# Two score steps in one: attention and feed-forward of 32 sequences on one core, with TensorE's order laid anew

## The reference

```
Q, K, V = x Wq' + bq, x Wk' + bk, x Wv' + bv          # 16 heads of 8 channels
scores  = Q K' / sqrt(8); above the diagonal -inf; plus -(i - j)
attn    = softmax(scores) V, then Wo and bo
x       = layernorm(x + attn)
h       = silu(w1 x * s1) * (w2 x * s2)               # 128 -> 512, ternary weights with a scale per row
h       = gelu(h1 h * s); h = gelu(h2 h * s)          # 512 -> 512, twice
x       = layernorm(x + w3 h * s)                     # 512 -> 128
```

## Time and profile before

| | |
|---|---|
| median of 3 executions | 780.16 us (778.53 to 780.32) |
| span of the profiled execution | 776.4 us |
| TensorE busy, share of the span | 729.4 us, 94% |
| VectorE | 598.0 us, 77% |
| ScalarE | 554.2 us, 71% |
| GpSimd | 509.5 us, 66% |
| mean granted TensorE clock | 0.959 |

### The profile page before, as it was taken

How to read it: one execution, slowest core, us unless ns; L and a number is a source line. 1 busy time by engine, 2 the same in 40 slices (tenths; PEclk the granted TensorE clock), 3 DMA queues, 4 the chain that set the end, 5 groups by cost and what they waited for, 6 DMA issues and landing times. The chain is left out here.

```text
span 776.4 us, 19033 instructions
## 1 busy us (share of the span) xinstructions
PE 729.4 (94%) x6025; PEld 497.7 (64%) x6025; DVE 598.0 (77%) x2759; ACT 554.2 (71%) x876; POOL 509.5 (66%) x616
## 2 busy tenths in 40 slices
PE   3798999999999999999999999999999999999895
PEld 1476466676766666676766667676766667676663
DVE  3978688797878889797888879797877979786242
ACT  5255558768595977869596877869596776959684
POOL 4145575858577585857677584857758585757764
PEclk8567899999999999999999999999999999999998
DMA  6511310303121120313122030312121030310100
GB/s 207 200 32 35 109 37 18 131 30 118 44 106 55 60 88 17 129 33 117 46 102 58 22 127 16 126 37 110 51 88 59 18 128 21 115 33 22 26 1 29
DMA packets 55213, 54.36 MB, mean 70 GB/s; under 512 B 27816, under 2 KB 35304, under 8 KB 55112
## 3 DMA queue, kind: packets, MB, share of 16 engines
q1 hardware_dynamic: 55112, 53.12, 21.0%
HBM read 12.20 MB, written 4.19 MB: 21 GB/s over the span
## 5 line engine op out<-in xcount | busy, mean ns | idle before, releaser
L969 DVE CUSTOM_DVE_ANT_0 ps<-ps,causal 128x256 f32<-128x256 f32 (+1 forms) x928 | 297.5, 393 | 26.1 <-PE ps L646 24.3
L1116 POOL TENSOR_SCALAR_AFFINE_SELECT pt<-pt 128x512 f32<-128x512 f32 x256 | 160.4, 636 | 105.0 <-ACT pt L819 100.0
L1163 POOL TENSOR_TENSOR hlo<-hf,hhi 128x512 fp32r<-128x512 f32 x128 | 164.0, 1287 | 95.7 <-ACT hhi L903 94.3
L819 ACT ACTIVATE pt<-ps 128x768 f32<-128x768 f32 x256 | 194.9, 808 | 31.1 <-PE ps L686 28.1
L893 ACT ACTIVATE hf<-ps,vec_sb 128x512 f32<-128x512 f32 x128 | 86.2, 684 | 99.6 <-PE ps L604 99.6
L598 PE MATMUL ps<-hhi,h_hi 128*128 128x512 f32 x496 | 146.3, 416 | 0.4 <-ACT hhi L903 0.3
L604 PE MATMUL ps<-hlo,h_hi 128*128 128x512 f32 x496 | 138.7, 398 | 1.7 <-POOL hlo L1169 0.7
L969 DVE DVE_READ_ACCUMULATOR2_ANT m<- 128x1 f32 x928 | 131.0, 141 | 0.0
L604 PEld LDWEIGHTS ps<-hlo,h_hi 128*128 128x128 f32 x496 | 93.4, 188 | 28.0 <-POOL hlo L1169 5.9
L703 PE MATMUL ps<-pt,vst 128*32 128x256 f32 (+1 forms) x2048 | 105.7, 335 | 0.1
L598 PEld LDWEIGHTS ps<-hhi,h_hi 128*128 128x128 f32 x496 | 85.3, 188 | 20.9 <-ACT hhi L903 0.7
(11 more groups left out here) (116 smaller groups left out, 1115.5 us busy)
## 6 DMA issues: line engine op xcount, KB each, us to landing
ks<-k_hi SPq DMA_DIRECT2D x30, 256.0 KB
qs<-q_hi SPq DMA_DIRECT2D x30, 256.0 KB
xT<-in_x SPq DMA_DIRECT2D x16, 256.0 KB, 2.8
x_tok<-in_xtok SPq DMA_DIRECT2D x16, 256.0 KB, 2.8
num<-raw SPq DMA_DIRECT2D x64, 64.0 KB, 2.0
den<-sums SPq DMA_DIRECT2D x128, 32.0 KB, 1.8
out<-o_tok SPq DMA_DIRECT2D x16, 256.0 KB, 2.2
ks<-k_lo SPq DMA_DIRECT2D x15, 256.0 KB
```

Of the source, the lines that this page charges most:

```text
L819: nc.scalar.activation(pt[u][:, c:c + 2, :], ps[:, first:last + 1, 0:3 * P], ACT.Exp).then_inc(t_free.sem, 1)
L969: part = nc.vector.tensor_tensor_reduce(ps[:, bank, cols], ps[:, bank, cols], mask, 1.0, LOWEST, ALU.add, ALU.max, m32[b][:, it, c + e, u: ...
L1116: nc.gpsimd.affine_select(out=diag, in_=diag, compare_op=ALU.is_ge, fill=0.0, base=0, pattern=[[0, 2], [0, 2], [1, P]], channel_multiplier ...
L1163: nc.gpsimd.tensor_tensor(h_lo[layer % 2][:, m, :], hf[:, n % 4, :], h_hi[layer % 2][:, m, :].bitcast(F32), ALU.subtract).then_inc(hlo_rea ...
```

## The change

Every even score step is joined with the next odd one. `s2` b, n stands for `s` n and n+1, `st2` b, n for `st` n and n+1. The four heads lie in four different groups of 32 partitions and four banks. All four wide products come first, then the four narrow ones; after the second narrow product the signal for step n is given, after the fourth that for n+1. Before the first product stands the wait that step n+1 had, so both pairs of banks must be free. In `st2` and also in the single `st` the wide product now comes before the narrow one. In the slot all 32 steps are joined to 16; in the fill some are. In `PE_ORDER` the other steps are placed anew around them: `h` 1,0 stands before `s2` 0,2, `mT` 0 behind `s2` 1,0, `x1t` directly behind `s2` 1,2, `qq` directly behind `s2` 1,4, and `pv` 0,2 and 0,3 side by side. Nothing is changed on the other engines.

```diff
 PE_ORDER = [
-    ("u", 3, -2), ("s", 0, 0, 0), ("s", 0, 1, 0), ("pv", 1, 2, -1), ("pv", 1, 3, -1), ("s", 0, 2, 0),
-    ("h", 1, 0, -2), ("s", 0, 3, 0), ("s", 0, 4, 0), ("h", 1, 1, -2), ("h", 1, 2, -2), ("s", 0, 5, 0),
-    ("s", 0, 6, 0), ("h", 1, 3, -2), ("s", 0, 7, 0), ("wo", -1), ("s", 1, 0, 0), ("h", 2, 0, -2), ("mT", 0, 0),
-    ("s", 1, 1, 0), ("s", 1, 2, 0), ("h", 2, 1, -2), ("s", 1, 3, 0), ("h", 2, 2, -2), ("s", 1, 4, 0),
-    ("s", 1, 5, 0), ("x1t", -1), ("h", 2, 3, -2), ("s", 1, 6, 0), ("s", 1, 7, 0), ("qq", 1), ("g", 0, -1),
-    ("u", 0, -1), ("w3h", -2), ("st", 0, 0, 0), ("st", 0, 1, 0), ("qk", 1), ("w3l", -2), ("st", 0, 2, 0),
-    ("st", 0, 3, 0), ("u", 1, -1), ("g", 1, -1), ("mT", 1, 0), ("st", 0, 4, 0), ("st", 0, 5, 0),
-    ("pv", 0, 0, 0), ("pv", 0, 1, 0), ("st", 0, 6, 0), ("st", 0, 7, 0), ("zt", 2, -2), ("g", 2, -1),
-    ("u", 2, -1), ("st", 1, 0, 0), ("st", 1, 1, 0), ("pv", 0, 2, 0), ("st", 1, 2, 0), ("g", 3, -1),
-    ("pv", 0, 3, 0), ("st", 1, 3, 0), ("st", 1, 4, 0), ("qv", 1), ("st", 1, 5, 0), ("pv", 1, 0, 0),
-    ("st", 1, 6, 0), ("st", 1, 7, 0), ("pv", 1, 1, 0),
+    ("u", 3, -2), ("s2", 0, 0, 0), ("pv", 1, 2, -1), ("pv", 1, 3, -1), ("h", 1, 0, -2), ("s2", 0, 2, 0),
+    ("h", 1, 1, -2), ("h", 1, 2, -2), ("s2", 0, 4, 0), ("h", 1, 3, -2), ("wo", -1), ("s2", 0, 6, 0),
+    ("h", 2, 0, -2), ("h", 2, 1, -2), ("s2", 1, 0, 0), ("mT", 0, 0), ("h", 2, 2, -2), ("s2", 1, 2, 0),
+    ("x1t", -1), ("h", 2, 3, -2), ("s2", 1, 4, 0), ("qq", 1), ("g", 0, -1), ("u", 0, -1), ("s2", 1, 6, 0),
+    ("w3h", -2), ("st2", 0, 0, 0), ("qk", 1), ("w3l", -2), ("st2", 0, 2, 0), ("u", 1, -1), ("g", 1, -1),
+    ("mT", 1, 0), ("st2", 0, 4, 0), ("pv", 0, 0, 0), ("pv", 0, 1, 0), ("st2", 0, 6, 0), ("zt", 2, -2),
+    ("g", 2, -1), ("u", 2, -1), ("st2", 1, 0, 0), ("pv", 0, 2, 0), ("pv", 0, 3, 0), ("st2", 1, 2, 0),
+    ("g", 3, -1), ("qv", 1), ("st2", 1, 4, 0), ("pv", 1, 0, 0), ("st2", 1, 6, 0), ("pv", 1, 1, 0),
 ]
...
-                        elif kind == "s":
+                        elif kind in ("s", "s2"):
                             _, b, n = s
-                            u, banks = n // 2, SCORE[n % 2]
+                            steps_of = (n,) if kind == "s" else (n, n + 1)
...
-                            wait_max_banks(pe, HP * b + n, q)
+                            wait_max_banks(pe, HP * b + steps_of[-1], q)
                             heads = []
-                            for e, bank in enumerate(banks):
-                                c = 2 * (n % 2) + e
...
+                            for i in steps_of:
+                                for e, bank in enumerate(SCORE[i % 2]):
+                                    c = 2 * (i % 2) + e
...
-                            for bank, qr, kr in heads:
-                                last = pe.matmul(ps[:, bank, T:T + P], qr[:, 0:P], kr[:, 0:P], start=False,
+                            for h, (bank, qr, kr) in enumerate(heads):
+                                part = pe.matmul(ps[:, bank, T:T + P], qr[:, 0:P], kr[:, 0:P], start=False,
                                                  stop=True, skip_group_check=True)
-                            last.then_inc(s_full.sem, 1)
+                                if h % 2:
+                                    part.then_inc(s_full.sem, 1)
...
-                        elif kind == "st":
+                        elif kind in ("st", "st2"):
...
-                            wait_exp_banks(pe, HP * b + n, q)
+                            wait_exp_banks(pe, HP * b + steps_of[-1], q)
...
-                                pe.matmul(ps[:, bank, 0:P], kr[:, P:T], qr[:, P:T], start=True, stop=False,
+                            for bank, qr, kr in heads:
+                                pe.matmul(ps[:, bank, P:P + T], kr[:, 0:P], qr, start=True, stop=False,
                                           skip_group_check=True)
-                                last = pe.matmul(ps[:, bank, P:P + T], kr[:, 0:P], qr, start=False,
+                            for h, (bank, qr, kr) in enumerate(heads):
+                                part = pe.matmul(ps[:, bank, 0:P], kr[:, P:T], qr[:, P:T], start=False,
                                                  stop=True, skip_group_check=True)
-                            last.then_inc(t_full.sem, 1)
+                                if h % 2:
+                                    part.then_inc(t_full.sem, 1)
```

More of the change, by code:

```diff
@@ L634, in run @@
                                 stacked.wait(pe, q - 1)
-                            wait_max_banks(pe, HP * b + n, q)
+                            wait_max_banks(pe, HP * b + steps_of[-1], q)
                             heads = []
-                            for e, bank in enumerate(banks):
-                                c = 2 * (n % 2) + e
-                                rows = slice(32 * c, 32 * c + 32)
-                                heads.append((bank, qs[p][rows, u, b * T:(b + 1) * T],
-                                              ks[p][rows, u, b * T:(b + 1) * T]))
+                            for i in steps_of:
+                                for e, bank in enumerate(SCORE[i % 2]):
+                                    c = 2 * (i % 2) + e
+                                    rows = slice(32 * c, 32 * c + 32)
+                                    heads.append((bank, qs[p][rows, i // 2, b * T:(b + 1) * T],
+                                                  ks[p][rows, i // 2, b * T:(b + 1) * T]))
                             for bank, qr, kr in heads:
@@ L672, in run @@
                             last.then_inc(mT_full.sem, 1)
-                        elif kind == "st":
+                        elif kind in ("st", "st2"):
                             _, b, n = s
-                            u, banks = n // 2, SCORE[n % 2]
+                            steps_of = (n,) if kind == "st" else (n, n + 1)
                             if n == 0:
                                 m_sent.wait(pe, q, 2 * b + 2)
-                            wait_exp_banks(pe, HP * b + n, q)
[L679 to L682, removed]
-                                pe.matmul(ps[:, bank, 0:P], kr[:, P:T], qr[:, P:T], start=True, stop=False,
+                            wait_exp_banks(pe, HP * b + steps_of[-1], q)
+                            heads = []
+                            for i in steps_of:
+                                for e, bank in enumerate(SCORE[i % 2]):
+                                    c = 2 * (i % 2) + e
+                                    rows = slice(32 * c, 32 * c + 32)
+                                    heads.append((bank, qs[p][rows, i // 2, b * T:(b + 1) * T],
+                                                  ks[p][rows, i // 2, b * T:(b + 1) * T]))
+                            for bank, qr, kr in heads:
+                                pe.matmul(ps[:, bank, P:P + T], kr[:, 0:P], qr, start=True, stop=False,
                                           skip_group_check=True)
-                                last = pe.matmul(ps[:, bank, P:P + T], kr[:, 0:P], qr, start=False,
+                            for h, (bank, qr, kr) in enumerate(heads):
+                                part = pe.matmul(ps[:, bank, 0:P], kr[:, P:T], qr[:, P:T], start=False,
                                                  stop=True, skip_group_check=True)
-                            last.then_inc(t_full.sem, 1)
+                                if h % 2:
+                                    part.then_inc(t_full.sem, 1)
                         elif kind == "pv":
```

## The result

The changed kernel takes 1002.27 us (median of 4, 999.89 to 1005.37) against 779.35 us: ratio 1.2865, 95% interval 1.2846 to 1.2885. It is slower by 223 us, as forecast in sign; the forecast was 976 us, the range 927 to 1018. The profiled execution has a span of 1003.7 us, 227.3 more than before.

What follows compares the result with a forecast made beforehand. TensorE, busy 43.56 of a slot's 44.11 us, was taken to bound the kernel, its order being the slot's length. Forecast: 776.4 span + 168 slot growth + 28 clock + 3.8 span to median = 976 us, range 927 to 1018.

Steps and rivals of the forecast that it cites:

- Adjacent steps overlap already: TensorE's score steps: two side by side start four wide products in 0.39 us, so joining saves only groups that stood alone.
- the 2.7 us: TensorE's saving per slot from fewer groups and wide first in `st`: up to 3.1 us, taken as 2.7.
- VectorE runs dry: Joined steps need both bank pairs free, so VectorE has nothing to read until they are through; idle eight times a slot.
- The bubble of 0.64 us: Delay from the start of a score product step to the start of its maxima on VectorE.
- the walk: Step-by-step timing of one slot from `s2` 0,0: it grows from 44.11 to 56.1 us, +168 over 14 slots.
- `x1t` and `qq` straight behind a score step: TensorE waits for VectorE's `mTl` 0 before `x1t`, 3.6 us, and for `x1lo` before `qq`, 3.4 us.
- `wo` waits for `arec` 1: `arec` 1 comes later on VectorE, then `spread` DMAs and POOL's product; TensorE waits 1.1 us before `wo`.
- The second half: From `st2` 0,0 on, exponentials on ScalarE hold up joined steps: 15.9 us against 14.49, growth 1.4 a slot.
- The clock: TensorE's granted clock falls around `x1t` and `h` 2,3: 2.45 us become about 4.45, +2.0 a slot, +28 in all.
- The second rival: Clock stays low beyond `h` 2,3 through `qq`, `g`, `u`, or falls twice: +49 us in all, 997 us; chance 0.24.
- The 3.8 us between span and median: Added to the whole kernel's forecast span because the median shown was 3.8 us above the span.
- The waits alone, without the clock: Rival where TensorE's clock stays high: slots grow only by the waits, 948 us; chance 0.25.

Runs made afterwards that it cites:

- two moves: Changed kernel with `s2` 1,4 moved ahead of `x1t` and `s2` 1,6 ahead of `qq`, everything still joined: 883.54 us, ratio 1.1337.
- the clock held up: Changed kernel plus 38 unread matmuls a slot in TensorE's four long gaps: 937.03 us; with `s2` 1,4 and `s2` 1,6 moved earlier and 17 extra matmuls: 864.59 us.

## Why the prediction was right, point by point

- **Adjacent steps overlap already, so joining saves only lone groups.** Shown: four heads take 0.39 us joined or side by side. With everything joined in the old order the kernel is slower by 84 us, so the up to 3.1 us a slot of removals did not come out on top. How much of the 2.7 us was really saved, no run shows by itself.
- **VectorE runs dry.** Shown: 233 us of idle before line 973, where there were 24.3, in seven places of a slot (I had said eight). The bubble of 0.64 us and the 1.25 us of a maxima step carried the walk to within 0.7 us at each point up to `x1t`.
- **`x1t` and `qq` straight behind a score step.** Shown as the largest part: 3.43 and 3.42 us measured for 3.6 and 3.4; two moves give 119 us back, 72 of them with the clock held up.
- **`wo` waits for `arec` 1.** Right in kind, 0.51 us measured for 1.1. TensorE was free at 11.7, as walked; the chain was quicker. From the first `spread` to POOL's product I had 4.41 us, now it is 3.93 (DMAs issued from 408.81), and POOL waits for the DMA: before, its product began (331.89) when the difference ahead of it ended (330.65 and 1.28 long), so that one had set the time and not the DMA. The row before and the row now:

```profile
330.65 1.28 POOL L1163 TENSOR_TENSOR hlo<-hf,hhi 128x512 fp32r<-128x512 f32 x1 [1.10 <-ACT hhi L903]
...
412.74 0.73 POOL L1147 TENSOR_TENSOR attT<-num,den 128x256 f32<-128x256 f32 x1 [1.19 <-DMA den<-sums]
```
- **The second half.** From `st2` 0,0 to the next slot the walk has 18.0 us; with the clock held up it took 17.68 (416.00 to 433.68). Joining `st` alone cost 1.4 us a slot, as walked.
- **The clock** was the mis-sized term. That it falls in every slot was right: `x1t` takes 1.11 to 1.12 us behind its wait in all 14 slots, 0.66 in the earlier trace rows. I had estimated it from one fall in the fill: 0.93 in the mean of the window from 66 to 68 us, with TensorE busy for 1.35 of 2.00 us, and 0.50 in the next, with TensorE busy in all of it. No trace of the kernel before or of the changed one shows the term as I had it, one fall a slot that ends behind `h` 2,3: the kernel before has no fall in its slots (1.00 in each half microsecond from 85.0 to 770.5), the changed one has two or three in each. I gave the fall 2.0 us a slot, `x1t` and `h` 2,3 alone. It measured 5.0 in the slots (60.45 in the mean against 55.46 with filled gaps), or 65 us / 14 = 4.7 by the times. In the slot shown, `x1t` and `h` 2,3 took 4.46 us (427.70 to 432.16) for 2.45, as priced. What I had put at nothing is the rest: `qq`, `g` 0 and `u` 0 took 3.71 (436.28 to 439.99) for 1.90; the second fall caught `qk` and `w3l`, so that `st2` 0,0 to 0,2 took 4.05 (443.65 to 447.70) for the 2.50 of the kernel with filled gaps (416.00 to 418.50); and three joined steps took 0.59 us for 0.39, each of which makes VectorE, and the wait behind it, some 0.25 us later. Together that is 6.1 us in this slot, one of the longer ones (61.46 us). The second rival, 997 us, priced `qq`, `g` 0 and `u` 0 as well, named a second fall, and came nearest. The step that failed took the clock as back at full speed behind `h` 2,3. A row against it was at hand: in the fill of the kernel before, the fall of the earlier trace rows at 68 us lasts until about 85, with 0.50 in each window from 68 to 84.
- **The 3.8 us between span and median** were too much. They set the span of one execution against the median of the others. Each profiled execution here takes 1.7 to 1.8 us more than its own span (1005.37 and 1003.7), so the forecast should have been some 2 us lower, further from the result.
- The waits alone, without the clock, I had at 948; measured 937. So part of the forecast's closeness is luck: a walk and a span term that were together 11 us too high made up for some of a clock term that was 37 us too small (28 against 65).

## What to carry to other kernels

Four banks filled together are one buffer, filled in pairs they are two: a joined step that saves issue time can take away the double buffering that keeps the reader at work, and the writer then waits for the reader's last read at each step. Where nothing else hung on it, that was about 0.5 us for a joined raw score step (60 us over 14 slots of 8). Whatever waits for the reader's side results belongs behind the next fill of its input, not before it; a wait costs least where the engine that is waited for has its next work in hand. And a gap on TensorE is paid twice where the clock falls in it (here 65 us over 14 slots): read the granted clock around each new wait, price everything until it is back, not only the step behind the gap, and look for a further fall behind the next wait.

## What the runs showed of the hardware

Products that nobody reads made a kernel faster: 38 extra ones a slot, 532 in all, took 65 us off. And the points at which the clock falls and comes back vary between slots of one execution. The same instructions make slots of 58.6 to 61.8 us; with the gaps filled they are 55.4 to 55.8. Two slots of the changed kernel that follow one another, from `x1t` on:

```profile
673.35 1.11 PE L728 MATMUL ps<-ident,x 128*128 128x128 f32 x4 [3.43 <-DVE mT_lo L999]
...
675.97 1.17 PE L601 MATMUL ps<-hlo,h_hi 128*128 128x512 f32 x4
...
680.93 2.07 PE L614 MATMUL ps<-xT,wq_sb 128*128 128x512 f32 x2 [3.42 <-DVE x1lo L1045]
```

```profile
734.59 1.91 PE L601 MATMUL ps<-hlo,h_hi 128*128 128x512 f32 x4
...
740.54 2.08 PE L614 MATMUL ps<-xT,wq_sb 128*128 128x512 f32 x2 [3.42 <-DVE x1lo L1045]
```

In the first the clock was back in the middle of `h` 2,3 (1.17 us for its last four products, 1.91 in the second) and fell a second time in the wait before `qq` (2.07 us for `qq`, 2.08 in the second). In windows of half a microsecond it is back at 676.0 in the first, 3.5 us after the fall, and at 744.5 in the second, 14 us after it. What decides between the two these traces don't show.
